# Decoder layer on one core: running sums of the linear attention as four 64x64 products per tile, and the residual X added by TensorE

## Chip, cores and metric

One core of a Trainium2 chip runs the whole program in one launch. The metric is the device time in microseconds (us) of that core.

## The reference, cut to what matters

A pre-norm decoder layer on x of 128 sequences of 64 tokens with 128 features: causal linear attention, then an attention by autocorrelation against a context, then a mixture of 8 experts with two chosen. Each adds its result to x. The change lies in the first part, which runs in one loop with the first half of the second:

```python
x = x + attn(layernorm(x));  x = x + xattn(layernorm(x), ctx, ctx);  x = x + moe(layernorm(x))
# attn, 16 heads of D = 8 features, for each sequence:
q = fmap(x @ wq + bq); k = fmap(x @ wk + bk); v = x @ wv + bv        # fmap(x) = x + 1 if x > 0 else exp(x)
step t:  S = S + outer(k[t], v[t]);  z = z + k[t]
         out[t] = (q[t] @ S) / (q[t] . z + 1e-6)
return out @ wo + bo
```

## The kernel before

A tile is 128 tokens (two sequences) on 128 partitions; there are 64 tiles in 16 groups of four. X stays in SBUF. The program is written by hand, engine by engine: each engine has a fixed order of instructions and meets the others through semaphores (`wait_ge`, `need`). The attention loop is software-pipelined: in slot n an engine works on group n+2 (stage a0: statistics and layer norm), n+1 (a1: projection, features, outer products), n (b: running sums, product with q), n-1 (c: division, output projection, sum into X, statistics) and n-2 (d: the second layer norm and the 64x64 correlation products, called gram here). `slots` (L309) runs n from -2 to 17, with the middle in a hardware loop of two slots.

What one slot does, with the lines of the profile:

- **PE** (TensorE): turns the normalised rows of a1 (`transposes` L1333, into bank 0), projects each of four tiles with one product of 384 columns (`project` L1344, q, k and v in bank 1), and takes the running sum over the tokens of each tile (`running_sums` L1336) as the product of `tri_s` (128x128, lower triangular within each sequence) with the outer products, 1152 columns in three pieces in banks 2, 3 and 4. Then `on` and `xh2` are turned in bank 5, `wkk` times the context goes to bank 7, the output projection and its bias to bank 6, and last the gram products (K = 128, each filling 64 of the 128 columns of the array, the two halves in turn) to bank 6.
- **ACT** (ScalarE): copies the turned tiles to SBUF (`xT` L640, `oT` L693, `x2T` L705), evacuates each projection in four steps (`a_evac_proj`: `ex` L647, `rl` L648, `v` L650, exponential L653), adds the epsilon to the denominators (`den` L658), does both layer norms (`nb` L668, `xh` L671), and copies `k2T` (L703) and the gram result `gd` (L719).
- **POOL** (GpSimd): sums ex and rl into the features `qk` (L534), forms the outer products (L542: v with a ninth column of ones, times k, so 16 x 9 x 8 = 1152 numbers per token; the ninth carries the sum of k for the denominator), and the roots of the variances (L526).
- **DVE** (VectorE): multiplies the running sums by q in three pieces per tile (`times_q` L896, `R`), sums over the 8 features (`sum_heads` L905, `nd`: numerator and denominator together), inverts the denominators (L930), divides (`quotients` L935, `on`), adds the attention into X (`add_attention` L943) and takes the statistics of both layer norms (L869, L877).

Three waits set much of the order: PE may write tile k+1's projection in bank 1 only when ACT has read tile k's (`a_pev`); PE may write a piece of the running sums only when DVE has multiplied the same piece of the tile before (`b_mul`); and ACT's queue is strictly in order, so that `oT` stands between two evacuations and waits for PE's transposes.

## Time and profile before

| | |
|---|---|
| Median of 3 runs | 631.92 us (631.75 to 633.5) |
| Span of the profiled execution | 631.7 us |
| Own time of that execution beside it | not listed apart; the shortest run is 631.75 us |
| Busy, PE / DVE / ACT / POOL | 91% / 82% / 67% / 68% |
| Attention loop | about the first 270 us |

Busy is the time in which an engine had at least one instruction in execution. Instructions of one engine overlap a little at their ends, so that the step from one start to the next is up to 0.1 us shorter than the duration printed. An fp32 product leaves two PE records, each of half its time.

### The profile page before, as it was taken

How to read it: one execution, taken by the hardware profiler on the slowest of the kernel's cores; microseconds unless marked ns; L12 is line 12 of the kernel's file. 1: busy time of each engine (PE TensorE's matmuls, PEld its weight loads, DVE VectorE, ACT ScalarE, POOL GpSimd, SP SyncE). 2: the span in 40 equal slices, each digit the busy share in tenths (PEclk: the TensorE clock that was granted, in tenths of full speed). 3: DMA queues.
4: the chain of work that ended last, by engine and by line, in shares of the span. 5: the costliest groups of instructions: out<-in, count | busy, mean ns of one | idle time of the engine just before them, and what ended most of it. 6: DMA issues, size and time to landing. Idle time of an engine off the chain costs nothing.

```text
span 631.7 us, 15833 instructions
## 1 busy us (share of the span) xinstructions
PE 575.6 (91%) x3838; PEld 442.8 (70%) x3839; DVE 517.9 (82%) x1602; ACT 420.2 (67%) x1188; POOL 427.0 (68%) x461
## 2 busy tenths in 40 slices
PE   3899999999999999968799877999999999999993
PEld 1455555555555555545689644799999999989993
DVE  5599999999999999983678888566877887877883
ACT  3557777877787777351788512345788888878882
POOL 2899989998999899310877600765467666757762
PEclk9999999999999999999999968899999999999998
DMA  5610111111161111283477551221012111111110
GB/s 147 184 51 0 35 33 35 34 33 33 33 100 33 34 33 34 66 119 90 119 208 202 113 113 29 53 51 46 27 49 54 48 47 47 51 38 51 51 44 23
DMA packets 49973, 40.92 MB, mean 65 GB/s; under 512 B 21971, under 2 KB 40278, under 8 KB 49926
## 3 DMA queue, kind: packets, MB, share of 16 engines
q1 hardware_dynamic: 44150, 29.61, 19.0%
q0 software_dynamic: 4960, 10.49, 6.4%
q8 instruction: 20, 0.33, 0.2%
q10 hardware_dynamic: 816, 0.26, 0.2%
q14 instruction: 27, 0.22, 0.1%
HBM read 27.47 MB, written 12.88 MB: 64 GB/s over the span
## 4 chain that ended last, share of the span: by engine, by line
PE 63%; ACT 12%; DVE 12%; issue 6%; DMA 4%; POOL 1%; DVEq 0%; ACTq 0%; SPq 0%; POOLq 0%
PE bank L1329 57%; PE bank L1333 4%; ACT xh L671 3%; ACT xs L773 2%; PE bank L1568 2%; DMA w_s<-gram_d 1%; DVE on L935 1%; ACT ex L647 1%; ACT nb_c L668 1%; DVE mean_early L1037 1%; DMA circ<-prob_d 1%; PE bank L1492 1%; ACT rl L648 1%; ACT xrT L759 1%; ACT ex L653 1%
## 5 line engine op out<-in xcount | busy, mean ns | idle before, releaser
L542 POOL TENSOR_TENSOR shared<-v,qk 128x1152 f32<-128x1152 f32 x64 | 142.8, 2231 | 2.8
L1329 PE MATMUL bank<-shared,tri_s 128*128 128x360 f32 (+1 forms) x384 | 137.2, 494 | 0.7 <-DVE R L896 0.7
L609 POOL DMA_INDIRECT shared<-xs_d,row_u x91 | 87.8, 964 | 62.2 <-DVE row_u L1227 31.6
L896 DVE TENSOR_TENSOR R<-bank,qk 128x360 f32<-128x360 f32 (+1 forms) x192 | 96.2, 540 | 8.6 <-PE bank L1329 6.7
L1329 PEld LDWEIGHTS bank<-shared,tri_s 128*128 128x128 f32 x384 | 69.8, 192 | 44.9 <-issue 20.4
L616 POOL DMA_INDIRECT out_x<-shared x64 | 63.6, 993 | 48.4 <-DVE shared L1299 21.8
L905 DVE TENSOR_REDUCE nd<-R 128x144 f32<-128x1152 f32 x64 | 86.1, 1346 | 1.6
L1329 PE MATMUL bank<-w_s,hid 128*128 (+1 forms) x620 | 82.3, 276 | 0.1
L1329 PEld LDWEIGHTS bank<-w_s,hid 128*128 128x128 f32 x620 | 75.5, 192 | 0.6 <-issue 0.3
L812 ACT ACTIVATE shared<-bank 128x256 f32<-128x256 f32 x155 | 59.4, 384 | 21.9 <-PE bank L1329 16.2
L1320 DVE TENSOR_TENSOR hid<-bank,shared 128x256 f32<-128x256 f32 x155 | 61.4, 422 | 10.0 <-ACT shared L812 9.8
L1329 PE MATMUL bank<-shared,ct 128*128 128x128 f32 x512 | 67.8, 275 | 0.0
L1329 PE MATMUL bank<-shared,u 128*128 128x128 f32 x512 | 67.6, 275 | 0.0
L1329 PE MATMUL bank<-wqkv,xT 128*128 128x384 f32 x128 | 56.7, 526 | 6.9 <-ACT v L650 4.6
L1329 PEld LDWEIGHTS bank<-shared,ct 128*128 128x128 f32 x512 | 62.2, 192 | 0.3 <-issue 0.2
L1329 PEld LDWEIGHTS bank<-shared,u 128*128 128x128 f32 x512 | 62.3, 192 | 0.0
L802 ACT ACTIVATE shared<-bank,scale_s 128x128 f32<-128x128 f32 (+1 forms) x78 | 30.1, 386 | 41.1 <-PE bank L1568 41.1
L534 POOL TENSOR_TENSOR qk<-ex,rl 128x256 f32<-128x256 f32 x64 | 48.0, 751 | 9.7 <-ACT ex L653 9.6
L647 ACT ACTIVATE ex<-bank 128x256 f32<-128x256 f32 x64 | 24.1, 376 | 36.2 <-PE bank L1329 36.2
L1329 PEld LDWEIGHTS bank<-wqkv,xT 128*128 128x128 f32 x128 | 22.5, 198 | 29.7 <-ACT v L650 21.6
L806 ACT ACTIVATE ct<-w_s 128x512 f32 x64 | 39.7, 620 | 0.1
L1329 PE MATMUL bank<-ones 128*128 128x512 bf16 x128 | 36.0, 423 | 0.0
(247 smaller groups left out, 1138.4 us busy)
## 6 DMA issues: line engine op xcount, KB each, us to landing
xs_d<-xs SPq DMA_DIRECT2D x16, 270.0 KB, 4.7
X<-in_x SPq DMA_DIRECT2D x16, 256.0 KB, 2.8
ct<-in_ctx_t SPq DMA_DIRECT2D x16, 256.0 KB, 2.8
ct<-in_ctx_r SPq DMA_DIRECT2D x16, 256.0 KB, 3.6
gram_d<-gd SPq DMA_DIRECT2D x14, 256.0 KB, 2.4
w_s<-in_w_experts SPq DMA_DIRECT2D x8, 384.0 KB, 4.0
circ<-prob_d SPq DMA_DIRECT2D x30, 64.0 KB, 2.7
shared<-xs_d,row_u POOLq DMA_INDIRECT x91, 2.6
```

The source lines that it names most:

```text
L534: nc.gpsimd.tensor_tensor(qk[p][:, k, :], ex[k % 2][:], rl[k % 2][:], ALU.add).then_inc(a_f, 1)
L542: nc.gpsimd.tensor_tensor(outer[k], v9[k % 2][:].unsqueeze(3).broadcast_to([P, H, D1, D]), kk.unsqueeze(2).broadcast_to([P, H, D1, D]), AL ...
L609: nc.gpsimd.indirect_dma_start(xg[q], None, xs_d[:, :], bass.IndirectOffsetOnAxis(ap=rows, axis=0)).then_inc(xg_in[q], 16)
L616: nc.gpsimd.indirect_dma_start(out[:, :], bass.IndirectOffsetOnAxis(ap=xg[(NXI + j) % NX][:, DEST:DEST + 1].bitcast(U32), axis=0), yg[q], ...
L647: nc.scalar.activation(ex[k % 2][:], bank[1][:, 0:2 * E], ACT.Relu, scale=-1.0).then_inc(a_pev, 1)
L802: nc.scalar.activation(xgT[p][:, cols], bank[0][:, cols], ACT.Copy, scale=scale_s[:, 0:1]).then_inc(x_xT, 1)
L806: nc.scalar.activation(w_tile[n % 2][0], w_s[:, dyn(held[0] * W_E, 2 * HID)], ACT.Copy).then_inc(x_wa, 1)
L812: nc.scalar.activation(silu[p][h], bank[1 + 2 * p + h][:, HID:2 * HID], ACT.Silu).then_inc(x_silu, 2 // len(items_of(i, up[0])))
L896: nc.vector.tensor_tensor(R[:, lo:hi], bank[2 + c][:, 0:n_h * D1 * D].rearrange("p (h e d) -> p h e d", h=n_h, e=D1), qq.unsqueeze(2).broa ...
L905: nc.vector.tensor_reduce(nd[p][:, k], R[:], AX.X, ALU.add).then_inc(b_red, 1)
L1320: nc.vector.tensor_tensor(hid[p][h][:], bank[1 + 2 * p + h][:, 0:HID], silu[p][h], ALU.mult).then_inc(x_h, 2 // len(items_of(i, j)))
L1329: return nc.tensor.matmul(o, l, r, start=start, stop=stop, skip_group_check=True)
```

## The change

It keeps the algorithm of the attention and its results, and lays it out otherwise:

- **Running sums**: the ones column goes. The outer product has 16 x 8 x 8 = 1024 numbers. The 128x128 triangular matrix is zero outside its two 64x64 diagonal blocks, so the product is written as four products of 64 rows by 64 columns, each with 512 columns of data. The first 512 columns (heads 0 to 7) go from token block 0 to 0 and 1 to 1, the other 512 (heads 8 to 15) from block 0 to 1 and 1 to 0. The result of a tile fills two banks, and there are two such pairs (`run0`, `run1`), used in turn.
- **Exchanged blocks**: for the heads 8 to 15, k and v are projected with the two sequences of the tile exchanged, so that the sums come out on the right partitions. `project` therefore has one product of 256 columns (v of heads 0 to 7, q, k of heads 0 to 7) and two of 64 tokens with 128 columns (k and v of heads 8 to 15).
- **Denominators**: `key_sums`, two PE products of 256 columns per group (keys of all four tiles times the triangular matrix, plain and exchanged), then on DVE a product with q (`key_dots`) and a sum (`sum_dots`).
- **X**: the identity times X (512 columns, fp32) is a further summand of the output projection in bank 6, and ACT copies the bank over X (`add_attention` on ACT); DVE's addition goes.
- **Banks**: the inverses `rden` lie in bank 6 and not in SBUF; `xT` is turned in bank 5; `wkk` times the context uses bank 4, which the key sums use too. `den` moves on ACT from the start of a slot to behind the third evacuation.

```diff
-D1 = D + 1
-        R = sb("R", [P, H, D1, D])
-        nd = [sb(f"nd{i}", [P, GT, H, D1]) for i in range(2)]
-        den, rden = sb("den", [P, GT * H]), sb("rden", [P, GT * H])
+        R = sb("R", [P, (D + 1) * E])
+        num = [sb(f"num{i}", [P, GT, E]) for i in range(2)]
+        zq = sb("zq", [P, GT * E])
+        den = sb("den", [P, GT * H])
...
+        run = [psum("run0", 2), psum("run1", 2)]
+        bank = [run[0][:, 0:512], psum("bank1"), run[1][:, 0:512], run[1][:, 512:1024], psum("bank4"), psum("bank5"),
+                psum("bank6"), run[0][:, 512:1024]]
+        rden = bank[6][:, 0:GT * H]
...
             def running_sums(g, p, r, k):
                 t = GT * g + k
                 pe.wait_ge(a_outer, t + 1)
-                for c, (lo, hi) in enumerate(HEADS):
-                    need(pe, b_mul, 3 * (t - 1) + c + 1)
-                    mm(bank[2 + c][:, 0:(hi - lo) * D1 * D], tri_s[:], outer[k][:, lo:hi].rearrange("p h e d -> p (h e d)")
-                       ).then_inc(b_run, 1)
+                need(pe, b_mul, t - 1)
+                settle(pe)
+                for c in range(2):
+                    for row in range(2):
+                        own, to = slice(row * L, row * L + L), (row + c) % 2 * L
+                        last = mm(run[k % 2][to:to + L, c * 512:c * 512 + 512], tri_s[own, own],
+                                  outer[k][own, c * 512:c * 512 + 512])
+                last.then_inc(b_run, 1)
+
+            def key_sums(g, p, r):
+
+                pe.wait_ge(a_f, GT * g + GT)
+                need(pe, b_dots, 2 * g - 1)
+                need(pe, d_kT, g - 2)
+                mm(bank[4][:, 0:GT * HALF], tri_s, qk[p][:, :, E:E + HALF])
+                mm(bank[4][:, GT * HALF:2 * GT * HALF], tri_f, qk[p][:, :, E + HALF:2 * E]).then_inc(b_keys, 1)
...
-                mm(bank[1][:, 0:3 * E], xT[:, k * P:(k + 1) * P], wqkv[:]).then_inc(a_proj, 1)
+                mm(bank[1][:, 0:2 * E], xT[:, k * P:(k + 1) * P], wqkv[:, 0:2 * E])
+                for h in range(2):
+                    last = mm(bank[1][h * L:h * L + L, 2 * E:3 * E], xT[:, k * P + (1 - h) * L:k * P + (1 - h) * L + L],
+                              wqkv[:, 2 * E:3 * E])
+                last.then_inc(a_proj, 1)
...
                     mm(bank[6][:], ones3[:], b_o, True, False)
+                    mm(bank[6][:], id_s[:], X[:, bass.ds(GT * g, GT), :], False, False)
...
+            def add_attention(g, p, r):
+                act.wait_ge(c_y, g + 1)
+                settle(act)
+                nc.scalar.activation(X[:, bass.ds(GT * g, GT), :].rearrange("p t e -> p (t e)"), bank[6][:], ACT.Copy
+                                     ).then_inc(c_x1, 1)
...
+            def key_dots(g, p, r):
+
+                dve.wait_ge(b_keys, g + 1)
+                nc.vector.tensor_tensor(
+                    zq[:].rearrange("p (k c x) -> p c k x", k=GT, c=2), bank[4][:].rearrange("p (c k x) -> p c k x", c=2, k=GT),
+                    qk[p][:, :, 0:E].rearrange("p k (c x) -> p c k x", c=2), ALU.mult).then_inc(b_dots, 1)
...
-            def add_attention(g, p, r):
-                dve.wait_ge(c_y, g + 1)
-                dve.wait_ge(a_xh, GT * g + GT)
-                xg = X[:, bass.ds(GT * g, GT), :]
-                nc.vector.tensor_tensor(xg, xg, bank[6][:].rearrange("p (t e) -> p t e", t=GT), ALU.add
-                                        ).then_inc(c_x1, 1)
```

How the rows move is shown at two places. The first is PE from the start of a slot (the transposes of `xh`) to the output projection in bank 6. Before:

```order
L1333 MATMUL bank0<-id_s,xh 128x128 x4
L1329 MATMUL bank2<-shared,tri_s 128x432
L1329 MATMUL bank3<-shared,tri_s 128x360
L1329 MATMUL bank4<-shared,tri_s 128x360
L1329 MATMUL bank1<-wqkv,xT 128x384
L1329 MATMUL bank7<-ct0,wkk 128x512
L1329 MATMUL bank1<-wqkv,xT 128x384
L1333 MATMUL bank5<-id_s,on 128x128 x4
```

And in the changed kernel:

```order
L1354 MATMUL bank5<-id_s,xh 128x128 x4
L1350 MATMUL run1<-shared,tris_s 64x512 x4
L1350 MATMUL bank1<-wqkv,xT 128x256
L1350 MATMUL bank1<-wqkv,xT 64x128 x2
L1350 MATMUL bank4<-qk1,tris_s 128x256 x2
L1350 MATMUL bank1<-wqkv,xT 128x256
L1350 MATMUL bank1<-wqkv,xT 64x128 x2
L1354 MATMUL bank5<-id_s,on 128x128 x4
L1350 MATMUL run0<-shared,tris_s 64x512 x4
L1350 MATMUL bank4<-ct1,wkk 128x512
L1350 MATMUL bank6<-bias3,ones3 128x512
L1350 MATMUL bank6<-X,id_s 128x512
```

Between the first two projections stand the key sums; the product with the context moves behind the second running sum, and the identity product joins the output projection.

The second place is ACT in the middle of a slot, from the second layer norm (`xh2`) to the fourth evacuation. Before:

```order
L671 ACTIVATE xh2<-X,nb_c0,rs_c0 128x128 x4
L703 ACTIVATE k2T<-bank7,wkk 128x512
L705 ACTIVATE x2T<-bank5 128x512
L647 ACTIVATE ex0<-bank1 128x256
L648 ACTIVATE rl0<-bank1 128x256
L650 ACTIVATE v9_0<-bank1 128x16x8
L653 ACTIVATE ex0<-ex0 128x256
```

And in the changed kernel:

```order
L685 ACTIVATE xh2<-X,nb_c0,rs_c0 128x128 x4
L715 ACTIVATE k2T<-bank4,wkk 128x512
L670 ACTIVATE X<-bank6 128x512
L720 ACTIVATE x2T<-bank5 128x512
L656 ACTIVATE ex0<-bank1 128x256
L657 ACTIVATE rl0<-bank1 128x256
L659 ACTIVATE v8_0<-bank1 128x128
L661 ACTIVATE ex0<-ex0 128x256
L665 ACTIVATE den<-den 128x64
```

The copy over X and the denominators now stand in a stretch in which ACT's queue had neither.

## Rows read from the trace of the kernel before

**Rows 1.** The page, section 1 (busy us, share of the span, instructions).

```profile
PE 575.6 (91%) x3838; PEld 442.8 (70%) x3839; DVE 517.9 (82%) x1602; ACT 420.2 (67%) x1188; POOL 427.0 (68%) x461
```

**Rows 2.** 13 slots: length, busy us of PE, PEld, DVE, ACT, POOL, clock, DMA.

```profile
37.93:238.92 200.99, 192.53 (x902) 114.00 (x901) 196.08 (x456) 152.99 (x510) 182.66 (x156) 1.00 0.14 34
```

**Rows 3.** Groups by form in these 13 slots: busy us, mean ns | idle before.

```profile
L542 POOL TENSOR_TENSOR shared<-v,qk 128x1152 f32<-128x1152 f32 x53 | 118.5, 2236 | 2.2
L905 DVE TENSOR_REDUCE nd<-R 128x144 f32<-128x1152 f32 x52 | 69.9, 1345 | 1.3
L896 DVE TENSOR_TENSOR R<-bank,qk 128x360 f32<-128x360 f32 x105 | 50.1, 517 | 0.0
L896 DVE TENSOR_TENSOR R<-bank,qk 128x432 f32<-128x432 f32 x52 | 30.2, 581 | 1.6 <-PE bank L1329 0.2
L943 DVE TENSOR_TENSOR X<-X,bank 128x512 f32 x10 | 6.8, 681 | 1.5 <-PE bank L1329 1.3
```

**Rows 4.** Waits in the same 13 slots: us in total, times, longest.

```profile
ACT ex L647 <- PE bank L1329: 24.7, 14, 2.2
ACT oT L693 <- PE bank L1333: 17.6, 13, 2.2
```

**Rows 5.** Timeline of ACT over one slot: start us, us, what [idle before].

```profile
129.54 0.59 ACT L640 ACTIVATE xT<-bank 128x512 f32<-128x512 f32 x1
130.03 0.31 ACT L658 ACTIVATE den<-nd 128x64 f32<-128x64 f32 x1
130.23 0.20 ACT L662 ACTIVATE mr_c<-mv_c 128x4 f32<-128x4 f32 x1
132.19 0.38 ACT L647 ACTIVATE ex<-bank 128x256 f32<-128x256 f32 x1 [1.76 <-PE bank L1329]
...
134.46 0.60 ACT L693 ACTIVATE oT<-bank 128x512 f32<-128x512 f32 x1 [1.14 <-PE bank L1333]
...
138.23 0.68 ACT L703 ACTIVATE k2T<-bank,wkk 128x512 f32<-128x512 f32 x1
139.08 0.60 ACT L705 ACTIVATE x2T<-bank 128x512 f32<-128x512 f32 x1 [0.17 <-PE bank L1333]
...
144.88 0.60 ACT L640 ACTIVATE xT<-bank 128x512 f32<-128x512 f32 x1
```

**Rows 6.** Timeline of PE in the same slot.

```profile
128.84 0.66 PE L1333 MATMUL bank<-id_s,xh 128*128 128x128 f32 x4
129.33 2.10 PE L1329 MATMUL bank<-shared,tri_s 128*128 128x432 f32 x6
131.27 0.81 PE L1329 MATMUL bank<-wqkv,xT 128*128 128x384 f32 x2
131.91 1.02 PE L1329 MATMUL bank<-ct,wkk 128*128 128x512 f32 x2
...
136.20 0.38 PE L1329 MATMUL bank<-bias,ones 128*128 128x512 bf16 x1
136.41 1.05 PE L1329 MATMUL bank<-wo_s,oT 128*128 128x128 f32 x8
```

**Rows 7.** Timeline of PE at the gram products, and a look at 143.51 us alone.

```profile
142.79 0.77 PE L1329 MATMUL bank<-shared,tri_s 128*128 128x360 f32 x2
143.49 0.69 PE L1329 MATMUL bank<-x2T,k2T 128*64 128x64 f32 x16
...
143.49 0.28 PE L1329 MATMUL bank<-x2T,k2T 128*64 128x64 f32 x2
```

**Rows 8.** The division on DVE: all 16 (min/median/max ns), one long one, POOL beside it.

```profile
L935 DVE TENSOR_TENSOR on<-nd,rden x16: 677/679/2592, 40.3 to 268.2; 128x512 f32<-128x512 f32 x16
...
147.40 2.59 DVE L935 TENSOR_TENSOR on<-nd,rden 128x512 f32<-128x512 f32 x1
...
147.26 2.18 POOL L542 TENSOR_TENSOR shared<-v,qk 128x1152 f32<-128x1152 f32 x1
```

**Rows 9.** The multiplications by q over eleven slots: min/median/max ns.

```profile
L896 DVE TENSOR_TENSOR R<-bank,qk x130: 487/522/608, 59.8 to 227.4; 128x360 f32<-128x360 f32 x87, 128x432 f32<-128x432 f32 x43
```

More of the change, by code:

```diff
@@ L236, in build, with psum @@
         y0 = sb("y0", [P, E])
-        bank = [ctx.enter_context(nc.psum_tensor(f"bank{i}", [P, 512], F32)) for i in range(8)]
+        def psum(name, banks=1):
+            return ctx.enter_context(nc.psum_tensor(name, [P, banks * 512], F32))
+        run = [psum("run0", 2), psum("run1", 2)]
+        bank = [run[0][:, 0:512], psum("bank1"), run[1][:, 0:512], run[1][:, 512:1024], psum("bank4"), psum("bank5"),
+                psum("bank6"), run[0][:, 512:1024]]
+        rden = bank[6][:, 0:GT * H]
         settled = sem("settled")
@@ L505, in _ @@
             pool.memset(power[:], -0.5).then_inc(setup, 1)
-            for k in range(2):
-                pool.memset(v9[k][:], 1.0).then_inc(setup, 1)
             pool.memset(ones_f[:], 1.0).then_inc(setup, 1)
@@ L636, in _ @@
         def _(act):
+            v_halves = bass.AP(bank[1][:].tensor, 0, [[512, P], [HALF + 2 * E, 2], [1, HALF]])
             def a_evac_xT(g, p, r):
@@ L639, in a_evac_xT @@
                 need(act, a_proj, GT * g)
-                nc.scalar.activation(xT[:], bank[0][:], ACT.Copy).then_inc(a_xT, 1)
+                nc.scalar.activation(xT[:], bank[5][:], ACT.Copy).then_inc(a_xT, 1)
             def a_evac_proj(g, p, r, k):
@@ L655, in denominators @@
             def denominators(g, p, r):
-                act.wait_ge(b_red, GT * g + GT)
-                need(act, c_rden, g)
-                nc.scalar.activation(den[:], nd[p][:, :, :, D].rearrange("p t h -> p (t h)"), ACT.Copy, bias=ATT_EPS).then_inc(c_den, 1)
+                act.wait_ge(b_dots, 2 * g + 2)
+                nc.scalar.activation(den[:], den[:], ACT.Copy, bias=ATT_EPS).then_inc(c_den, 1)
+            def add_attention(g, p, r):
[3 more added lines that the diff above has]
+                                     ).then_inc(c_x1, 1)
             def negative_mean(g, p, mv, mv_sem, mr, mr_sem):
@@ L674, in slot @@
             def slot(n, i):
-                a0, a1, c, d = (stage(n, i, s) for s in (2, 1, -1, -2))
+                a0, a1, b, c, d = (stage(n, i, s) for s in (2, 1, 0, -1, -2))
                 if i is None and n == 1:
                     act.wait_ge(kk_mm, 1)
-                    nc.scalar.activation(wkk[:], bank[7][:, 0:E + 1], ACT.Copy).then_inc(kk_w, 1)
+                    nc.scalar.activation(wkk[:], bank[6][:, 0:E + 1], ACT.Copy).then_inc(kk_w, 1)
                 if i is None and n == NG:
@@ L702, in slot @@
                     need(act, d_gram, d[0])
-                    nc.scalar.activation(k2T[:], bank[7][:], ACT.Identity, bias=wkk[:, E:E + 1]).then_inc(d_kT, 1)
+                    nc.scalar.activation(k2T[:], bank[4][:], ACT.Identity, bias=wkk[:, E:E + 1]).then_inc(d_kT, 1)
+                if c:
+                    add_attention(*c)
+                if d:
                     act.wait_ge(d_tr, d[0] + 1)
@@ L707, in slot @@
                     a_evac_proj(*a1, 2)
+                if b:
+                    denominators(*b)
                 if a0:
@@ L916, in step @@
                     dve.wait_ge(fold_ch, n)
-                step(nc.vector.tensor_copy(vo_f[:], bank[0][0:3, 0:E]))
+                step(nc.vector.tensor_copy(vo_f[:], bank[4][0:3, 0:E]))
                 step(nc.vector.tensor_copy(vo_p[0][:], vo_f[:]))
@@ L965, in slot @@
                     sum_heads(*b, 1)
+                    sum_dots(*b)
                 if a0:
@@ L1370, in slot @@
                     need(pe, a_xT, a1[0])
-                    transposes(bank[0], xh).then_inc(a_tr, 1)
+                    need(pe, d_xT, a1[0] - 3)
+                    transposes(bank[5], xh).then_inc(a_tr, 1)
                 if b:
@@ L1377, in slot @@
                     project(*a1, 0)
-                if d:
-                    g, p, r = d
-                    pe.wait_ge(ct_in[p], 16 * r + 16)
-                    need(pe, d_kT, g)
-                    if i is None and g == 0:
-                        pe.wait_ge(kk_w, 1)
-                    mm(bank[7][:], wkk[:, 0:E], ct[p][:]).then_inc(d_k, 1)
+                if b:
+                    key_sums(*b)
                 if a1:
@@ L1396, in slot @@
                     running_sums(*b, 2)
+                if d:
+                    g, p, r = d
+                    pe.wait_ge(ct_in[p], 16 * r + 16)
+                    need(pe, d_kT, g)
+                    if i is None:
+                        need(pe, b_dots, 2 * min(g + 2, NG - 1) + 1)
+                    else:
+                        pe.wait_ge(b_dots, 2 * (g + 2) + 1)
+                    if i is None and g == 0:
+                        pe.wait_ge(kk_w, 1)
+                    if i is None and n == NG:
+                        pe.wait_ge(fold_ch, 1)
+                    mm(bank[4][:], wkk[:, 0:E], ct[p][:]).then_inc(d_k, 1)
                 if c:
```

122 lines of the change are left out of this document (64 added, 58 removed).

## The prediction

> **What bounds the kernel now.** I read the page first, then the busy time of the attention loop, the groups and the waits in it, and last the timelines of one slot. Over the whole span no engine is full [rows 1]. In the attention loop all are near it: the 13 slots between two xT copies take 200.99 us, 15.46 us each, of which DVE is busy 196 us, PE 193, POOL 183 and ACT 153 [rows 2]. So a lighter DVE or PE is worth something only as far as the next queue lets it, and I look for the loop of dependences that closes a slot. In ACT's timeline one slot runs from xT at 129.54 to xT at 144.88, 15.34 us, in three stretches [rows 5]: 2.65 us from xT to `ex` with 1.76 idle, 2.27 us from `ex` to `oT` with 1.14 idle, and 10.42 us from `oT` to the next xT with almost no gap. Both idle times are waits for PE, and the waits of all slots say the same: 24.7 and 17.6 us, and nothing longer on ACT [rows 4]. ACT is the emptiest engine by busy time, and yet its queue is closed but for two latencies. PE is the other party: its own work in a slot, below, is 14.3 us.
>
> **PE, if the four quadrants run side by side.** Both passes of an fp32 product cost 1.94 us for 1152 columns, 0.64 for 384 (129.33 to 131.27, 131.27 to 131.91) [rows 6], 1.68 ns a column. Transposes of four tiles take 0.49. A slot before: 4 x 1.94 + 4 x 0.64 + 3 x 0.49 + 0.86 (context) + 0.21 (bias) + 0.9 (output projection) + 0.6 (gram) = 14.4 us. Now: a running sum lasts as long as 512 columns, 0.86. Whether halves of the array overlap is shown for columns alone: at 143.51, two gram records are under way, both begun at 143.49, and 16 records of 64 columns last 0.69 us with their tail, where 16 x 0.054 one after another would be 0.86 before the tail [rows 7]. Halves by rows stand nowhere in this trace. From below the price is 0.86 us (all four at once), from above 3.44 (none). I take 0.86, since the gram rows are the nearest and show the array divided, with both fp32 passes in step. Each change of the array's division costs about 0.10 us: the product of 2 x 360 columns at 142.79 has streamed out at 143.39, and gram begins at 143.49 [rows 7]. I charge 0.2 to each running sum and 0.2 to each projection (256 columns 0.43, two of 128 side by side 0.21). Added are the key sums, 0.86, and the identity times X, 0.86. Sum: 4 x 1.06 + 4 x 0.84 + 1.72 + 1.47 + 0.86 + 0.21 + 0.9 + 0.6 = 13.4 us. PE gains 1.0 us a slot in spite of 1.72 us of new products.
>
> The Trainium skill speaks against this price: "TensorEngine Tiling (Array Packing)", section Restrictions and Gotchas, says that row tiles write to different PSUM banks and cannot be in the same bank at once. Here blocks 0 and 1 of one half of the columns write the same bank, in different partitions, so that by the rule at most two of the four would run together. No row here decides it; it is the first rival.
>
> **DVE.** Multiplication by q: three pieces per tile, 2 x 0.517 + 0.581 = 1.61 us [rows 3]; one of 1024 columns at the slope between the two forms (0.064 us for 72 columns, 0.89 ns) is 0.58 + 0.53 = 1.11. Saved 0.5 a tile nominally; the pieces overlap by some 0.08 at each end, so I take 0.35, 1.4 a slot. Sum over features: 1345 ns for 1152 numbers [rows 3], 1.20 for 1024, saves 0.6 a slot. The addition into X goes, 0.68. Added: key dots, 512 columns from PSUM like that addition, 0.68, and their sum at the rate of the reduction, 0.6. Net -1.4 us: from 15.1 to 13.7 us a slot. **The division** is a case of its own: it lasts 0.68 us but up to 2.59, and the long one, begun at 147.40, ends at 149.99 after waiting for a POOL product that began at 147.26 and ends at 149.44 [rows 8]. The 130 multiplications with one operand in PSUM, under way beside the same POOL products, never last over 0.61 us [rows 9]. With the inverses in PSUM the division becomes of that kind, and I expect it never to be long. This is what makes the mean slot 15.46 where the one shown has 15.34.
>
> **POOL.** The outer product shrinks from 1152 to 1024 columns: 2.24 to 1.99 us [rows 3], 1.0 us a slot, from 14.1 [rows 2] to 13.1. Nothing is added.
>
> **ACT.** New is the copy over X, 0.49 us (as xT, 129.54 to 130.03). Between `k2T` and `x2T` there are 0.85 us now, 0.36 more than such a copy takes, since `x2T` waits for PE's transposes [rows 5]; the copy fills that hole and costs 0.14. `den` costs 0.20 (130.03 to 130.23) and moves from a place that was hidden by the wait for `ex` into the closed stretch: +0.20. It waits for DVE's `sum_dots`, in DVE's queue behind the second sum, some 4 us earlier in the slot: no wait. The X copy waits for the output projection, which PE ends before ACT has finished `xh2`; behind it stand `x2T`, the gram products and DVE's statistics of X, the last the ones to suffer if it is late. The evacuations keep their sizes.
>
> **The sum, along ACT.** Stretch one: xT copy 0.60, projection 0.43 + 0.21 + 0.1, end to `ex` 0.28 (131.91 to 132.19): 1.65; the running sum before it may still be under way, so 1.8 instead of 2.65. It was held up by the 1.94 us running sum. Stretch two: 2.27 + 0.2 for the divided projection = 2.45. Stretch three: 10.42 + 0.14 + 0.20 = 10.75. Together 15.0 us a slot instead of 15.46; with DVE at 13.7, PE at 13.4 and POOL at 13.1, ACT's loop comes last. 13 slots x 0.46 = 6.0 us, and three partly filled slots around them at 0.3, 0.9 us. The remaining 360 us, the prologue and the second half, have the same work. Span 631.7 - 6.9 = 624.8, and the runs' median lies 0.2 above the span: **625 us**. Bounds of the unknown: if switching the array's division is free and the two small waits of stretch three vanish, 14.5 us a slot, 617; if each stretch keeps 0.2 of wait, 15.3, 629.
>
> **Rivals.**
> 1. *Only two quadrants at a time (or the passes in turn).* By a PSUM bank that takes one row half at a time, a running sum costs 1.72 + 0.2; PE needs 13.4 + 4 x 0.86 = 16.8 us a slot and is the bound. 13 x (16.8 - 15.46) + 3 x 1.4 = +21.6: **653 us**, slower. It decides as soon as a running sum lasts over 1.45 us. Against it the gram rows; for it that no row shows halves by rows. With all four in turn, 3.64 a tile, PE needs 23.7 a slot: some 760 us.
> 2. *ACT's queue swallows the gain.* PE's relief doesn't reach `ex` and `oT` sooner, because PE's transposes of `xh` or the DVE division come late, and the waits of 1.76 and 1.14 us stay. Then a slot is 15.34 + 0.34 + 0.2 = 15.9: 13 x 0.4 + 3 x 0.4 = +6.5, **638 us**, slower. For it: ACT has no other gap. Against: the running sum that stands ahead of the projection halves.
> 3. *More is freed.* The waits for PE shrink further and the slot falls to the needs of DVE and PE with some 0.5 us of latency, 14.2: 13 x 1.26 + 3 = 19 us, **612 us**. ACT's own work is 153 / 13 = 11.8 us, now 12.3 [rows 2], which allows it; its two round trips to PE speak against it.
> 4. *The change moves nothing*, 632: gains and new work cancel in the loop.
>
> **Chances.** My forecast (617 to 629) 0.50; rival 3, 0.14; rival 4, 0.06; rival 2, 0.10; rival 1, 0.20, of which 0.03 for all in turn. About 0.3% (1.9 us) is what a measurement of this kernel can tell from no change. Faster: 0.50 + 0.14 + 0.01 = 0.65; same 0.07; slower 0.10 + 0.20 less the part of rival 2 that ends near 632, 0.28. The range takes in all but rival 1: 609 to 640.
>
> **What the changed kernel's profile would show.** Four running-sum products (8 records) of one tile begun within some 0.45 us and followed 0.9 to 1.1 us later by the projection: right; 1.9 us later: rival 1. ACT's idle before `ex` at 0.9 us instead of 1.76, and before `oT` at 1.3. Every division at about 0.7 us. The copy over X with no idle before it over 0.2. DVE busy 13.7 of 15.0 us, no longer 15.1 of 15.46. The forecast is wrong if PE stays busy without a gap, or if ACT's idle before `ex` stays over 1.5 us, or if the time moves outside the first 270 us.

## The result, and the profile after

| | before | after |
|---|---|---|
| device time, median of 6 runs each | 633.19 us (631.75 to 634.38) | 636.0 us (635.08 to 637.61) |
| ratio, 95% interval | 1 | 1.0043 [1.0025, 1.006] |
| the profiled execution: time, span | 633.5, 631.7 us | 636.48, 634.5 us |
| 13 slots of the attention loop | 200.99 us, 15.46 each [rows 2] | 202.36 us, 15.57 each |

The change makes the kernel 0.4% slower. The forecast was 625 us, faster. The time lies outside the 617 to 629 us that had a chance of 0.50, inside the wide range of 609 to 640, and on the other side of no change.

The span grew by 2.8 us: 1.37 in the 13 slots, 0.38 before the first of them (38.31 against 37.93), 1.05 between the last slot and the end, the last groups of the loop among it. Where less work takes longer is a question for the loop, so its rows come first. The page, section 1, as [rows 1]:

```profile
PE 568.0 (90%) x4318; PEld 413.2 (65%) x4319; DVE 499.0 (79%) x1490; ACT 425.9 (67%) x1204; POOL 407.6 (64%) x459
```

The 13 slots in the columns of [rows 2], and then two of their groups by form as in [rows 3]:

```profile
38.31:240.67 202.36, 186.91 (x1299) 90.41 (x1291) 181.45 (x366) 157.19 (x523) 167.62 (x157) 1.00 0.14 34
```

```profile
L549 POOL TENSOR_TENSOR shared<-v,qk 128x1024 f32<-128x1024 f32 x53 | 103.5, 1953 | 2.2
L909 DVE TENSOR_TENSOR R<-run,qk 128x1024 f32<-128x1024 f32 x53 | 64.2, 1212 | 7.8 <-PE run L1350 6.4
```

Every engine but ACT has less to do, and ACT, with 0.3 us more, is the emptiest: a slot now holds 14.4 us of PE (186.91 / 13; 14.8 before), 13.96 of DVE (15.1), 12.9 of POOL (14.1), 12.1 of ACT (11.8). No engine is full, and yet the slot is longer, so load doesn't set it.

The mean hides part of the loss. Before, 3 of the 13 slots held a division of over 2.5 us [rows 8]; one of them is the slot from xT at 144.88 [rows 5] to the next xT:

```profile
161.31 0.59 ACT L640 ACTIVATE xT<-bank 128x512 f32<-128x512 f32 x1
```

That is 16.43 us; the other two such slots have 16.2 and 16.4, and the eight around them, from the third slot on, 15.2 to 15.4. In the changed kernel no division is long, and from the third slot on each lasts 15.5 to 15.7. So those three slots gave back 2.1 us, and the other ten lost 3.4.

The waits of the same 13 slots, ACT's and one of DVE for ACT (us in total, times, longest):

```profile
ACT oT L705 <- PE bank L1354: 19.8, 13, 1.9
ACT ex L656 <- PE bank L1350: 15.7, 13, 1.2
DVE st_c L886 <- ACT X L670: 11.6, 12, 1.1
...
ACT x2T L720 <- PE bank L1354: 5.6, 12, 0.5
```

The wait for `ex` fell from 24.7 to 15.7 us [rows 4], as foreseen in direction (1.23 us in the slot below; 0.9 was forecast); that of `x2T` is now 0.5 us in 12 slots. The timeline of ACT over the same piece of a slot as [rows 5]:

```profile
131.23 0.59 ACT L649 ACTIVATE xT<-bank 128x512 f32<-128x512 f32 x1
...
133.14 0.38 ACT L656 ACTIVATE ex<-bank 128x256 f32<-128x256 f32 x1 [1.23 <-PE bank L1350]
...
135.72 0.60 ACT L705 ACTIVATE oT<-bank 128x512 f32<-128x512 f32 x1 [1.44 <-PE bank L1354]
...
139.48 0.68 ACT L715 ACTIVATE k2T<-bank,wkk 128x512 f32<-128x512 f32 x1
140.05 0.59 ACT L670 ACTIVATE X<-bank 128x512 f32 x1
141.15 0.60 ACT L720 ACTIVATE x2T<-bank 128x512 f32<-128x512 f32 x1 [0.50 <-PE bank L1354]
...
146.87 0.59 ACT L649 ACTIVATE xT<-bank 128x512 f32<-128x512 f32 x1
```

The three stretches of the prediction are 1.91, 2.58 and 11.15 us, together 15.64; forecast were 1.8, 2.45 and 10.75, and before they were 2.65, 2.27 and 10.42. The first gave 0.74 of the 0.85 forecast. The third lost 0.73. Between the starts of `k2T` and `x2T` it lost 0.82 (0.85 before, 1.67 now, and 1.58 to 1.67 in all 12 of the 13 slots that have the two), where the prediction added 0.14; the rest of the stretch gave 0.09 back. `x2T` waits for PE, so PE's timeline of that stretch is next:

```profile
134.02 1.07 PE L1350 MATMUL bank<-wqkv,xT 128*128 128x256 f32 x6
135.02 0.66 PE L1354 MATMUL bank<-id_s,on 128*128 128x128 f32 x4
135.61 1.09 PE L1350 MATMUL run<-shared,tris_s 64*64 64x512 f32 x8
136.63 1.12 PE L1350 MATMUL bank<-ct,wkk 128*128 128x512 f32 x2
137.59 0.38 PE L1350 MATMUL bank<-bias,ones 128*128 128x512 bf16 x1
137.81 1.02 PE L1350 MATMUL bank<-X,id_s 128*128 x2
138.66 1.05 PE L1350 MATMUL bank<-wo_s,oT 128*128 128x128 f32 x8
139.56 0.97 PE L1350 MATMUL bank<-wqkv,xT 128*128 128x256 f32 x6
140.45 0.66 PE L1354 MATMUL bank<-id_s,xh 128*128 128x128 f32 x4
```

(The printed duration of a PE row runs up to 0.17 us into the next one, so PE is read here from start to start.) From the second projection at 134.02 to the transposes of `xh2` at 140.45 there is no idle time: 6.43 us in which PE does what stands in its order. ACT's `xh2`, whose last piece overlaps the start of `k2T` at 139.48 a little, was done at 139.59. The transposes come 0.86 us after that, because the third projection, begun at 139.56, stands ahead of them, and it could begin no sooner for the products ahead of it. The same piece before, and the wait of PE for `xh` in all 13 slots:

```profile
133.07 0.91 PE L1329 MATMUL bank<-wqkv,xT 128*128 128x384 f32 x2
133.82 0.60 PE L1333 MATMUL bank<-id_s,on 128*128 128x128 f32 x4
134.26 2.10 PE L1329 MATMUL bank<-shared,tri_s 128*128 128x432 f32 x6
...
137.31 0.81 PE L1329 MATMUL bank<-wqkv,xT 128*128 128x384 f32 x2
138.39 0.66 PE L1333 MATMUL bank<-id_s,xh 128*128 128x128 f32 x4 [0.27 <-ACT xh L671]
```

```profile
PE bank L1333 <- ACT xh L671: 3.3, 12, 0.3
```

Here PE had nothing left to do and waited 0.27 us for `xh`, as in all 12 slots that have these transposes: ACT came last. Start to start, with 0.64 for the last projection [rows 6], PE's row took 4.88 us, and the transposes began 5.32 us after the second projection, so PE had 0.44 us of room. By PE's row is meant, from here on, this sequence from the second projection to the transposes of `xh2`. The difference of the two rows, 1.55 us, is the sum of: second projection +0.25, transposes of `on` +0.15, running sum -0.92, context product +0.96 (moved in), identity product +0.85, third projection +0.25, and 0.01 for the rest. PE's total fell, and its row in the one place where the slot is closed grew.

**The theory** I took into the experiments, called P in the expectations: the slot is closed at the transposes of `xh2`, by the later of two rows. ACT's goes from the second projection over `ex`, `v`, `oT`, the third evacuation and the shifts `nb_c` to `xh2`; PE's is the one above. The rivals are named in the expectations: that ACT's queue, with the copy over X, closes the slot (A), and that only the sum of PE's work counts or that the layout gains nothing (Q).

**The four quadrants** were the open price, and the trace settles it. A look at 130.53 us alone:

```profile
130.50 0.66 PE L1350 MATMUL run<-shared,tris_s 64*64 64x512 f32 x4
```

All four 64x64 products of the first pass are under way at once, begun within 20 ns (0.64 us each, 0.66 together), and a running sum takes 1.02 us start to start (135.61 to 136.63), not 3.44. Two of them write into the same PSUM bank, in different partitions. By the Trainium skill, "TensorEngine Tiling (Array Packing)", section Restrictions and Gotchas, they could not have run together; for blocks in different partitions of one bank the measurement differs, and decides.

### The profile page after: what moved, and what is told of

It reads as the page before. It is cut to its first block, busy times and chain, and to the rows that moved or that the text cites. A ratio compares the mean times of both kernels' runs of the same rounds, so it can differ in the third digit from the quotient of the medians.

```text
span 634.5 us, 16770 instructions
## 1 busy us (share of the span) xinstructions
PE 568.0 (90%) x4318; PEld 413.2 (65%) x4319; DVE 499.0 (79%) x1490; ACT 425.9 (67%) x1204; POOL 407.6 (64%) x459
## 4 chain that ended last, share of the span: by engine, by line
PE 65%; ACT 12%; DVE 8%; issue 7%; DMA 4%; POOL 3%; ACTq 1%; SPq 0%; DVEq 0%; POOLq 0%
PE bank L1350 37%; PE run L1350 22%; PE bank L1354 3%; ACT xh L685 2%; ACT xs L790 2%; PE run L1618 2%; DMA w_s<-gram_d 2%; ACT ex L656 1%; ACT nb_a L681 1%; DVE mean_early L1058 1%; ACT xT L649 1%; PE run L1542 1%; ACT ex L661 1%; DMA ct<-in_ctx_r 1%; POOL shared L549 1%
## 5 line engine op out<-in xcount | busy, mean ns | idle before, releaser
L549 POOL TENSOR_TENSOR shared<-v,qk 128x1024 f32<-128x1024 f32 x64 | 125.0, 1952 | 2.8
L909 DVE TENSOR_TENSOR R<-run,qk 128x1024 f32<-128x1024 f32 x64 | 77.6, 1213 | 15.5 <-PE run L1350 14.0
L1350 PE MATMUL bank<-wqkv,xT 128*64 128x128 f32 (+1 forms) x384 | 70.5, 353 | 15.3 <-ACT v L659 10.6
L919 DVE TENSOR_REDUCE num<-R 128x128 f32<-128x1024 f32 x64 | 77.3, 1208 | 1.6
L1350 PE MATMUL run<-shared,tris_s 64*64 64x512 f32 x512 | 72.3, 636 | 0.0
L540 POOL TENSOR_TENSOR qk<-ex,rl 128x256 f32<-128x256 f32 x64 | 46.6, 728 | 12.9 <-DVE mv_a L894 7.5
L1350 PE MATMUL run<-w_s,hid 128*128 (+1 forms) x312 | 41.4, 275 | 0.0
L1350 PE MATMUL bank<-w_s,hid 128*128 (+1 forms) x308 | 41.0, 276 | 0.3 <-issue 0.3
L1350 PEld LDWEIGHTS run<-w_s,hid 128*128 128x128 f32 x312 | 38.0, 192 | 0.1
L1350 PEld LDWEIGHTS bank<-w_s,hid 128*128 128x128 f32 x308 | 37.5, 192 | 0.7 <-issue 0.5
L829 ACT ACTIVATE shared<-bank 128x256 f32<-128x256 f32 x77 | 29.6, 384 | 10.3 <-PE bank L1350 8.1
L1350 PE MATMUL run<-shared,ct 128*128 128x128 f32 x256 | 34.0, 276 | 0.1
```

Source lines behind the costliest of these rows:

```text
L540: nc.gpsimd.tensor_tensor(qk[p][:, k, :], ex[k % 2][:], rl[k % 2][:], ALU.add).then_inc(a_f, 1)
L549: nc.gpsimd.tensor_tensor(outer[k].rearrange("p (h e d) -> p h e d", h=H, e=D), vv.unsqueeze(3).broadcast_to([P, H, D, D]), kk.unsqueeze(2 ...
L829: nc.scalar.activation(silu[p][h], bank[1 + 2 * p + h][:, HID:2 * HID], ACT.Silu).then_inc(x_silu, 2 // len(items_of(i, up[0])))
L909: nc.vector.tensor_tensor(R[:, 0:D * E].rearrange("p (h e d) -> p h e d", h=H, e=D), run[k % 2][:].rearrange("p (h e d) -> p h e d", h=H, ...
L919: nc.vector.tensor_reduce(num[p][:, k, :], R[:, 0:D * E].rearrange("p (x d) -> p x d", d=D), AX.X, ALU.add).then_inc(b_red, 1)
L1350: return nc.tensor.matmul(o, l, r, start=start, stop=stop, skip_group_check=True)
```

## The experiments

Each kernel ran beside the kernel before on the same chip, whose median was 633.2 to 633.5 us each time; there are 4 to 6 runs of each, 12 of e5. Ratios are to those runs. The slot is the mean of 13, from the first xT to the fourteenth in the profile. `id·X` is the identity product.

| run | edit | us (median) | ratio to before, 95% | slot |
|---|---|---|---|---|
| after | | 636.0 | 1.0043 [1.0025, 1.006] | 15.57 |
| e1 | after, DVE adds X, no id·X | 627.08 | 0.9894 [0.9871, 0.9916] | 14.89 |
| e2 | after, DVE copies the bank over X | 636.16 | 1.0047 [1.0029, 1.0065] | 15.63 |
| e3 | before, with id·X and ACT's copy | 638.04 | 1.0077 [1.005, 1.0104] | 15.67 |
| e4 | after, `nb_c` before `oT` | 636.11 | 1.0047 [1.0031, 1.0063] | 15.61 |
| e5 | after, PE turns `xh2` before the 3rd projection | 630.21 | 0.9944 [0.9925, 0.9964] | 15.14 |
| e6 | after, undivided projection, blocks not exchanged | 625.53 | 0.9878 [0.9848, 0.9907] | 14.92 |
| e7 | e1 and e4 | 624.34 | 0.9852 [0.982, 0.9885] | 14.78 |
| e9 | e7, four pieces moved | 623.2 | 0.9832 [0.981, 0.9854] | 14.32 |
| e10 | e9, old order in the last groups | 618.44 | 0.976 [0.9738, 0.9782] | 14.31 |
| e8 | e10 without `nb_c` early | 628.34 | 0.9917 [0.9892, 0.9941] | 14.99 |
| e11 | before, `nb_c` before `oT` | 626.43 | 0.9897 [0.9874, 0.9921] | 14.95 |

### e1: the addition back on DVE

```diff
-                    mm(bank[6][:], id_s[:], X[:, bass.ds(GT * g, GT), :], False, False)
...
-                if c:
-                    add_attention(*c)
...
+                nc.vector.tensor_tensor(xg, xg, bank[6][:].rearrange("p (t e) -> p t e", t=GT), ALU.add
+                                        ).then_inc(c_x1, 1)
```

> The changed kernel without its last part: no identity product on PE, X is added by DVE behind the third multiplication by q, as before the change. Theory P (PE's own row of work between the second projection and the transposes of xh2 closes the slot, and the 0.86 us identity product stands in it): a slot falls from 15.64 to about 14.9 us, 13 slots and three partial ones give about -11 us, 625 us. Rival A (ACT's queue, which got the copy over X, closes the slot): the copy is gone as well, 0.5 to 0.8 us a slot, 625 to 629 us; this run doesn't part P from A. Rival Q (quadrants and divided projection cost what they save): nothing gained, 634 to 637 us.

Measured: 627.08 us, 9 less than after, and a slot of 14.89 us as P had it; A allowed this time too. The timeline where the slot is closed:

```profile
137.28 0.68 ACT L715 ACTIVATE k2T<-bank,wkk 128x512 f32<-128x512 f32 x1
...
137.44 0.65 PE L1361 MATMUL bank<-id_s,xh 128*128 128x128 f32 x4
...
138.13 0.60 ACT L718 ACTIVATE x2T<-bank 128x512 f32<-128x512 f32 x1 [0.17 <-PE bank L1361]
```

`k2T` to `x2T` is 0.85 us again, as before the change. The layout without the X part (quadrants, divided projection, separate denominators with their inverses in PSUM) is worth 6.3 us; putting X into the bank turns that into a loss. Both halves of that step, the product and the copy, went here, so the next runs separate them.

### e2: the product stays, DVE copies

```diff
-                if c:
-                    add_attention(*c)
...
+            def add_attention(g, p, r):
+                dve.wait_ge(c_y, g + 1)
+                dve.wait_ge(a_xh, GT * g + GT)
+                nc.vector.tensor_copy(X[:, bass.ds(GT * g, GT), :], bank[6][:].rearrange("p (t e) -> p t e", t=GT)
+                                      ).then_inc(c_x1, 1)
```

> The changed kernel with the identity product kept and the copy of bank 6 over X made by DVE instead of ACT. Theory P: x2T on ACT still waits for PE's transposes of xh2, which stand behind the identity product, so k2T to x2T stays at 1.6 to 1.7 us, and the slot at 15.5 to 15.7 us: 634 to 637 us. Rival A: 0.5 us a slot is won on ACT, slot 15.1, 628 to 629 us.

Measured: 636.16 us, no different from after. ACT's waits in the 13 slots:

```profile
ACT x2T L718 <- PE bank L1360: 11.4, 12, 1.0
```

Without its copy ACT waits twice as long at `x2T` (11.4 us, 5.6 in after) and reaches it no sooner. The copy on ACT lies beside PE's lateness and costs nothing here; A falls for the changed kernel.

### e3: the identity product and the copy in the kernel before

```diff
+                    mm(bank[6][:], id_s[:], X[:, bass.ds(GT * g, GT), :], False, False)
...
-                nc.vector.tensor_tensor(xg, xg, bank[6][:].rearrange("p (t e) -> p t e", t=GT), ALU.add
-                                        ).then_inc(c_x1, 1)
...
+                nc.scalar.activation(X[:, bass.ds(GT * g, GT), :].rearrange("p t e -> p (t e)"), bank[6][:], ACT.Copy
+                                     ).then_inc(c_x1, 1)
```

> The kernel before with only the X part of the change: identity product on PE, copy over X on ACT, no addition on DVE; running sums, projection and denominators as before. Theory P: PE had 14.4 us of work in a slot of 15.46 and now has 15.3; the slot becomes 16.3 to 16.5 us, about +14 us, 647 us. Rival A: the copy fills the hole before x2T, +0.14 to +0.5 us a slot, 635 to 640 us.

The edit also takes over the changed kernel's extra semaphore steps (`settle`) in the layer norm; `xh2` lasts 1.65 us with and without them. Measured: 638.04 us, 4.7 more than before, where P had forecast 14. Where ACT and PE meet:

```profile
139.01 0.68 ACT L710 ACTIVATE k2T<-bank,wkk 128x512 f32<-128x512 f32 x1
...
139.58 0.59 ACT L663 ACTIVATE X<-bank 128x512 f32 x1
139.59 0.60 PE L1334 MATMUL bank<-id_s,xh 128*128 128x128 f32 x4
...
140.23 0.60 ACT L715 ACTIVATE x2T<-bank 128x512 f32<-128x512 f32 x1
```

P's number came from adding 0.86 us to PE's total as if PE were full. It isn't. Reckoned as a row, PE has 0.44 us of room and gets 0.85 more, so the slot should grow by 0.41; and the slots without a long division, from the third on, are 15.65 to 15.72 us, against 15.2 to 15.4 before. The mean grew by 0.21 only, since the first two slots grew less and the longest slots shrank: there are five long divisions here (2.2 to 2.3 us) in place of three, but the slots that hold them last 15.8 to 16.0. The sign was right and the reckoning was the prediction's own mistake again, load in place of a row. In this kernel the copy on ACT and PE's transposes end together, at 140.17 and 140.19, and `x2T` follows at 140.23; which of the two holds it can't be told.

### e4: the shifts of the second layer norm before `oT`

```diff
+                if d:
+                    shifts(... nb_c ...)
                 if c:
                     act.wait_ge(c_tr, c[0] + 1)
...
-                    norm(... nb_c and xh2 ...)
+                    norm(... xh2 alone ...)
```

> The changed kernel with four small ACT instructions (the shifts nb of the second layer norm, 0.74 us in all) moved from behind the third evacuation into ACT's idle time before oT. Nothing else moves. Theory P: xh2 is ready 0.7 us sooner, but PE reaches its transposes no sooner; ACT only waits longer before x2T: 15.5 to 15.7 us a slot, 634 to 637 us. Rival A (ACT's queue closes the slot by its work): -0.74 us a slot, 624 to 627 us.

Measured: 636.11 us, unchanged, as P had it. ACT over the middle of a slot:

```profile
136.87 0.60 ACT L709 ACTIVATE oT<-bank 128x512 f32<-128x512 f32 x1 [0.72 <-PE bank L1359]
...
141.09 0.60 ACT L670 ACTIVATE X<-bank 128x512 f32 x1 [0.50 <-PE bank L1355]
142.30 0.60 ACT L724 ACTIVATE x2T<-bank 128x512 f32<-128x512 f32 x1 [0.62 <-PE bank L1359]
```

The four shifts do fill the hole before `oT` (0.72 us of idle instead of 1.44), and most of it comes back as waits for PE, 0.50 us at the copy and 0.62 at `x2T`, where there were 0.50 in all. Shortening ACT's row is worth nothing while PE's is the later one.

### e5: two pieces of PE's order exchanged

```diff
-                if a1:
-                    project(*a1, 2)
                 if d:
                     pe.wait_ge(d_xh, GT * g + GT)
                     transposes(bank[5], xh2).then_inc(d_tr, 1)
+                if a1:
+                    project(*a1, 2)
```

> The changed kernel, identity product kept, with PE's transposes of xh2 ahead of the third projection instead of behind it. Theory P: xh2 is ready when the output projection ends, so x2T starts about 0.6 us sooner; the third projection, 0.6 us later, then makes ACT wait some 0.2 us before the third evacuation. Slot 15.64 to 15.25 us, 13 slots -5 us: 630 to 632 us. Theory Q (the identity product only fills PE, its place is indifferent): 635 to 637 us.

Measured over 12 runs: 630.21 us (627.97 to 633.48), 5.8 less than after, with the same instructions. PE, and ACT at `x2T`:

```profile
136.63 1.05 PE L1350 MATMUL bank<-wo_s,oT 128*128 128x128 f32 x8
137.61 0.66 PE L1354 MATMUL bank<-id_s,xh 128*128 128x128 f32 x4
138.10 0.97 PE L1350 MATMUL bank<-wqkv,xT 128*128 128x256 f32 x6
```

```profile
138.50 0.60 ACT L720 ACTIVATE x2T<-bank 128x512 f32<-128x512 f32 x1
```

This is the plainest proof of P: no product removed, none shortened, and the loss is a gain of 0.6% (P had 630 to 632 us). `x2T` waits no more; the transposes stand one projection earlier. `k2T` begins at 137.45, so `k2T` to `x2T` is 1.05 us with the copy between them and no wait.

### e6: the projection undivided

```diff
-                mm(bank[1][:, 0:2 * E], xT[:, k * P:(k + 1) * P], wqkv[:, 0:2 * E])
-                for h in range(2):
-                    last = mm(bank[1][h * L:h * L + L, 2 * E:3 * E], ...)
-                last.then_inc(a_proj, 1)
+                mm(bank[1][:, 0:3 * E], xT[:, k * P:(k + 1) * P], wqkv[:]).then_inc(a_proj, 1)
```

> The changed kernel with the projection as one product of 384 columns, without exchanged token blocks; heads 8 to 15 then take k and v of the other sequence of the tile, which this kernel leaves wrong. It prices the divided projection: 1.0 us against 0.64. Theory P: it stands in ACT's wait before ex, in the one before oT and twice in PE's row before the transposes of xh2, so a slot loses 0.36 in each of three stretches: 14.5 to 14.7 us, -13 to -15 us, 622 us. Theory Q (only PE's total load counts): PE is busy 14.4 of 15.6 us and waits anyway, under 3 us.

This kernel leaves out the exchange of the two sequences, so that its heads 8 to 15 get the k and v of the other sequence of the tile: it gives a price and isn't a version to use. Measured: 625.53 us, and 14.92 us a slot. So the divided projection costs 0.65 us a slot, less than the 0.9 to 1.1 that P had and far more than Q's. In PE's row:

```profile
136.22 0.81 PE L1350 MATMUL bank<-wqkv,xT 128*128 128x384 f32 x2
136.87 0.60 PE L1354 MATMUL bank<-id_s,xh 128*128 128x128 f32 x4
137.40 1.09 PE L1350 MATMUL run<-shared,tris_s 64*64 64x512 f32 x8
```

0.65 us start to start for 384 columns, against 0.89 and 1.00 divided, and the transposes behind an undivided product take 0.53 (136.87 to 137.40), against 0.59. Four times 0.3 would be 1.2 us; it is P's reading, not shown apart, that only the projections in the closing row count at their full length.

### e7: e1 and e4 together

> Run e1_dve_adds (slot 14.85) with the four shifts nb of the second layer norm moved into ACT's idle time before oT. Theory P: x2T still waits for PE, which is busy without a gap from the second projection to the transposes of xh2, so nothing is won: 624 to 628 us. Rival A: ACT is now the bound, -0.74 us a slot, 615 to 618 us.

Measured: 624.34 us, 2.7 less than e1, with overlapping runs (621.58 to 628.37 against 623.7 to 627.75) and 0.1 us a slot. It lies in P's range, and rival A (615 to 618) is out. Its `x2T` waits 10.3 us in 12 slots, e1's 2.0: ACT is ahead now and PE closes the slot. One more step needs a shorter row of PE.

### e9, e10, e8: PE's row emptied

e9 takes e7 and moves four pieces. On PE the key sums go from between the first two projections to behind the last running sum, and the context product takes their place, out of the row; on DVE `key_dots` and `sum_dots` go to the end of the slot; on ACT `den` goes back before `ex`.

```diff
                     project(*a1, 0)
-                if b:
-                    key_sums(*b)
+                if d:
...
+                    mm(bank[4][:], wkk[:, 0:E], ct[p][:]).then_inc(d_k, 1)
                 if a1:
                     project(*a1, 1)
...
                     running_sums(*b, 3)
+                    key_sums(*b)
```

> Run e1_dve_adds with PE's row shortened as well: key sums moved into PE's idle time before the fourth projection, the context product back between the first and second projection, key dots and their sum at the end of DVE's slot, den back into ACT's idle time before ex, and the shifts nb before oT. Theory P: PE's row before the transposes of xh2 loses 0.96 us, ACT's stretch 0.74 + 0.15, the slot falls from 14.85 to 14.0 to 14.3 us, where DVE (13.9 us busy) is next: 614 to 619 us. If neither row closes the slot, no change against e1: 625 us.

Measured: a slot of 14.32 us, at the upper end of what P had, and 623.2 us, which is outside (614 to 619). From the last xT to the end it took 398.5 us, 6.7 more than in e7 (391.8). PE in the two last groups, and the busy time of the stretch 248 to 266 us in the columns of [rows 2]:

```profile
250.56 0.23 PE L1361 MATMUL bank<-bias,ones 128*128 128x128 bf16 x1 [2.06 <-DVE zq L928]
253.40 2.04 PE L1361 MATMUL bank<-ct,wkk 128*128 128x512 f32 x2 [2.11 <-DVE vo_f L947]
```

```profile
248.00:266.00 18.00, 12.36 (x64) 6.17 (x60) 10.48 (x40) 6.77 (x21) 3.45 (x6) 0.81 0.55 79
```

The key dots that moved to a slot's end have no next slot to hide in there, and the context product, in its new place, waits for folded biases that DVE makes late. PE stood still for 4.2 us, and the granted clock of this stretch was 0.81, so that part of it ran at the lower of the two levels, 1.2 GHz and not 2.4: the context product at 253.40 took 2.04 us, and 1.12 in the changed kernel's loop. e10 keeps the order of the changed kernel in the last two groups:

```diff
+                if b and i is None and n == NG - 1:
+                    key_sums(*b, last=True)
...
+                if b and not (i is None and n == NG - 1):
+                    key_sums(*b)
```

> Run e9_rearranged with the old order in the last two groups (key sums early, context product behind the running sum, denominators in the same slot). In e9 the slot was 14.34 us on average, but from the last xT copy to the end it took 398.5 us, where e7_dve_adds_nb_early took 391.8: the last slots wait for the late denominators and for the folded biases. Theory P: the slots stay at 14.3 and the rest returns to 392: 615 to 618 us. If the order of the last slots is not the cause, 622 to 624 us.

Measured: 618.44 us, 2.4% less than the kernel before, the fastest of this study, just above the 615 to 618 expected. From the last xT to the end it takes 393.45 us, and its slot is 14.31. The 13 slots:

```profile
36.76:222.85 186.09, 174.47 (x1273) 85.41 (x1265) 184.55 (x378) 150.65 (x509) 166.24 (x156) 1.00 0.15 37
```

DVE is busy 184.55 of 186.09 us, 99% (98% before, 90% in the changed kernel). Load now leaves next to nothing to win by a change of order; that it is what sets the slot is argued from this share, no run lightened DVE alone. The 1.7 us that the tail still has over e7's weren't looked into.

e8 is e10 without the early shifts, to see what they are worth once PE's row is short.

> As e10_tail_kept, but with the shifts nb of the second layer norm left behind the third evacuation. PE's row is shortened, ACT's stretch is not, but for den (0.15 us). Theory P, by which the longer of the two closes the slot: x2T comes no later than in e10 by more than what ACT lacks, 0.4 to 0.7 us a slot: 14.6 to 14.8 us, 620 to 624 us. If ACT's stretch is indifferent, as e10: 615 to 618 us.

Measured: 628.34 us, 9.9 more than e10, and the waiting has changed sides:

```profile
134.73 0.66 PE L1367 MATMUL bank<-id_s,xh 128*128 128x128 f32 x4 [0.92 <-ACT xh L685]
```

PE waits 0.92 us for ACT's `xh`. The same edit, four shifts a slot earlier, is worth 0.0 us a slot in the changed kernel (e4), 0.1 with DVE's addition (e7), and 0.67 here. Expected were 14.6 to 14.8 us a slot and 620 to 624: the direction held, the size didn't. And e8 is no faster than e1 (627.08): the four pieces moved on PE, DVE and ACT win nothing either while ACT's row is the later one.

### e11: the control, only the shifts moved in the kernel before

> Control: the kernel before, with nothing but the shifts nb moved into ACT's idle time before oT. Theory P: PE's work of 14.4 us a slot, DVE's 15.1 and PE's row before the transposes of xh2 stand as before; ACT only waits longer before x2T: within 0.3% of before, 631 to 635 us. Rival: the rearrangement of ACT alone wins what the later versions show, 0.5 us a slot, 625 to 627 us.

Measured: 626.43 us, 6.9 less than before. P's own expectation was wrong and the rival's right. ACT at `x2T`, and the divisions as in [rows 8]:

```profile
135.93 0.60 ACT L709 ACTIVATE x2T<-bank 128x512 f32<-128x512 f32 x1 [0.42 <-PE bank L1338]
```

```profile
L940 DVE TENSOR_TENSOR on<-nd,rden x16: 677/679/1459, 40.1 to 261.6; 128x512 f32<-128x512 f32 x16
```

By P's own mechanism it should have been foreseen: in the kernel before PE waits 0.27 us for `xh`, so ACT's row is the later one, and an edit that shortens it must pay. It pays 0.51 us a slot, until PE is later (`x2T` now waits 0.42). That is more than the 0.27, and the trace has the rest. None of its 13 slots holds a long division (the one of 1.46 us comes after them), so that the three slots of 16.2 to 16.4 us fell to 14.9 to 15.0: 4.2 of the 6.7 us won in 13 slots. The other ten gave 2.5, about 0.3 each from the third on, which is the wait. The divisions got short here with both operands still in SBUF, by coming a little earlier than POOL's product: the one at 129.62 us stands before the product at 129.85.

Of the 14.9 us that e10 gains, 6.9 are thus to be had without the change, and no less than the 6.3 of e1's whole new layout. e7 is 2.1 us faster than e11 with overlapping intervals; e10 goes clearly beyond it.

## Why the prediction was wrong

**Right, by its steps.** The four quadrants run together: 1.02 us a running sum, 1.06 forecast, and rival 1 is out. DVE at 13.96 (13.7 forecast; a multiplication by q took 1.21 and not 1.11) and POOL at 12.9 (13.1) fell about as reckoned. Stretch one, 1.91 us (1.8), and the wait for `ex`, which fell by 9 us. The copy over X costs 0.20 us where nothing else is late (e5: 1.05 against 0.85), 0.14 forecast. The division is never long, though POOL's product is under way beside it:

```profile
L964 DVE TENSOR_TENSOR on<-num,bank x16: 674/676/686, 41.3 to 269.9; 128x512 f32<-128x512 f32 x16
...
132.78 1.96 POOL L549 TENSOR_TENSOR shared<-v,qk 128x1024 f32<-128x1024 f32 x1
...
133.28 0.68 DVE L964 TENSOR_TENSOR on<-num,bank 128x512 f32<-128x512 f32 x1
```

Up to 2592 ns before [rows 8], 686 now, with one operand in PSUM. Of the 16 divisions 14 began while a product of POOL was under way and none waited; before, exactly the four that began so were long. It agrees with the Trainium skill, "SBUF — State Buffer", section SBUF: two separate sides, by which VectorE and GpSimd exclude each other for a whole instruction where VectorE reads two operands from SBUF or runs in a two-port mode.

**Luck.** That e1, without the X part, gains 6.3 us, close to the 6.9 forecast for the whole, is chance: it keeps DVE's addition, which the forecast had taken away, and 4.3 of the 7.4 us that it gains in 13 slots lie in the three that a long division had stretched.

**The step that failed** is in the paragraph on ACT: "The X copy waits for the output projection, which PE ends before ACT has finished `xh2`", and the copy "fills that hole and costs 0.14". The output projection did end in time, at 139.56. But the hole before `x2T` was one of waiting for PE's transposes, and these stand behind the output projection and the third projection. The prediction had put the identity product, the context product and the divided projections into PE's total, found it 1.0 us lower, and asked no more of PE than that; it did not ask where in PE's order they stand. Reckoned as a row from the second projection, its own prices gave 0.20 + 0.20 + 0.86 + 0.86 - 0.88 = +1.24 us, against 0.44 of room and the 0.20 of divided projection by which ACT's row grows too: 0.6 us late. Measured, it is 1.55 - 0.44 - 0.30 (ACT's row from the second projection to `k2T`, 5.16 us before and 5.46 after) = 0.81, and 0.82 is what `k2T` to `x2T` grew by. e5 shows the step alone: the same products, with the transposes one place earlier, and 5.8 us less. The prices for the right answer were in the text; the 0.44 of room was not among its rows, but stood in the same trace. What I said would prove the forecast wrong, PE busy without a gap, is what happened in that stretch.

**Sizes.** The forecast missed by 11.0 us (636.0 against 625), 9.7 of them in the span. The other 1.3 are its term "the runs' median lies 0.2 above the span": the median then was 631.92 against a span of 631.7, but the profiled execution itself took 633.5, and with six runs the medians lie 1.5 above the spans, before and after. The slot of the timelines is 15.64 us, 0.64 over the forecast: 0.40 in stretch three, 0.13 in stretch two, 0.11 in stretch one. In stretch three the hole took 0.68 more than foreseen, and `den` (0.15, not 0.20) and the evacuations after `x2T` gave 0.28 back. Over 13 mean slots it is 7.4 us ((15.57 - 15.0) x 13). The other 2.3 of the 9.7 us lie in the partly filled slots and what follows: 0.9 of gain forecast, 1.4 of loss found (0.38 + 1.05). PE was also undersized, 14.4 us a slot and not 13.4: a divided projection takes 0.89 to 1.00 (0.84), the context 0.96 (0.86), the key sums 1.07 (0.86), four transposes behind a divided product 0.59 (0.49).

**The rivals.** Rival 2, 638 us, is the nearest by time, and half right: the gain was swallowed in the queue order. But it named ACT's queue and the waits for `ex` and `oT`. The wait for `ex` fell, and by e2 and e4 less work in ACT's queue wins nothing in the changed kernel; the order that swallowed the gain is PE's. The wait for `oT` did stay (17.6 and 19.8 us), and e4 shows that removing half of it changes nothing. Rival 3, a slot at DVE's need, was out of reach for the change as made; e10 gets to it with the order rearranged.

## What to carry to other kernels

In a pipelined loop over several engines, an engine that is 92% busy need not be the bound, and one that loses work can still make the loop longer. Find the instruction at which the slot is closed, list what stands ahead of it on both engines since their last meeting, and put each added or moved product into that row before it goes into a total. An edit that shortens the earlier row is worth nothing and looks useless, until the later one is shortened; the same four shifts were worth 0.0, 0.1, 0.5 and 0.7 us a slot in four surroundings. Try such a move in the old kernel first: here it won as much as the new layout. A move within the loop is also to be followed through its last turn, where there is no next slot to cover it (6.7 us in e9).

## What the runs showed of the hardware

- Four fp32 products of 64x64, two of them into one PSUM bank, ran at the same time; the first pass of all four began within 20 ns, and both passes of 512 columns took 1.02 us, against 0.85 for one undivided product of 512 columns (identity times X, 137.81 to 138.66).
- Dividing a product has a price of its own: 0.89 to 1.00 us for 256 columns and two of 128 side by side, 0.65 for 384 undivided, though the columns that stream are the same 384.
- The change of division is paid on both sides. Four transposes took 0.44 to 0.49 us between undivided products, 0.47 to 0.52 behind divided gram products and before undivided running sums, 0.53 the other way round (e6), and 0.59 between two divided ones.
- A multiplication on DVE with one operand in PSUM was never lengthened by a GpSimd product under way (14 divisions begun beside one, 686 ns at most; [rows 9] for the multiplications by q before). With both operands in SBUF the four divisions begun beside one took 1.39 to 2.59 us, and the others 0.68 to 0.69 [rows 8].
